# Two attention layers on one core: stacks of 28 rows in four row groups, and scores of one four of heads set beside the transposed scores of the one before

## The reference, cut to what matters

```python
xn = _layernorm(x)
x = x + attention0(xn) + quantized_ffn(xn)      # biases; 128 -> 512 -> 128 with gelu, blocks of 32 rounded to 3 bits
xn = _layernorm(x)
x = x + attention1(xn) + moe(xn)                # 8 experts, 128 -> 512 -> 128, silu(x wg) * (x wu) @ wd, all summed
# attention: sim = q k^T / sqrt(8), causal;  e = exp(sim - max);  out = (e v) / sum(e);  out @ Wo
```

## Time and profile before

| | us |
|---|---|
| runs | 1624.28, 1640.37, 1633.93; median 1633.93 |
| the profiled execution | 1633.84 |
| its span | 1632.1 |
| its mean granted PE clock | 0.914 of 2.4 GHz |
| PE busy | 1501.3 (92%) |
| PEld / DVE / ACT / POOL busy | 840.4 / 1036.6 / 823.3 / 678.2 |

### The profile page before, as it was taken

The page is one execution under the profiler, slowest core; times in us unless marked ns, Lnnn a source line. Parts: engine busy times, 40 slices in busy tenths (PEclk is TensorE's granted clock), DMA queues, the critical chain, the costliest instruction groups (busy, mean ns, idle before and its releaser), DMA issues. The chain is left out here.

```text
span 1632.1 us, 23537 instructions
## 1 busy us (share of the span) xinstructions
PE 1501.3 (92%) x8440; PEld 840.4 (51%) x8440; DVE 1036.6 (64%) x2379; ACT 823.3 (50%) x1220; POOL 678.2 (42%) x791
## 2 busy tenths in 40 slices
PE   2899999999999999369999999999999999999987
PEld 1444444444444443245656656666666566666655
DVE  3545655565655453157876767777777677777743
ACT  2335455555545445135655556555655565555650
POOL 4222324243333223245554455454545554545440
PEclk9559888898979789679999999999999999999997
DMA  3312223232413221231010110111111101111003
GB/s 118 85 35 74 73 82 93 68 98 71 125 56 106 79 64 61 72 92 54 28 52 27 31 47 28 34 48 36 32 53 32 43 28 35 32 37 32 18 14 111
DMA packets 59025, 93.95 MB, mean 58 GB/s; under 512 B 12119, under 2 KB 22876, under 8 KB 56862
## 3 DMA queue, kind: packets, MB, share of 16 engines
q1 hardware_dynamic: 57902, 92.00, 18.9%
q10 hardware_dynamic: 1008, 0.46, 0.1%
HBM read 50.08 MB, written 40.11 MB: 55 GB/s over the span
## 5 line engine op out<-in xcount | busy, mean ns | idle before, releaser
L1133 POOL TENSOR_TENSOR a_h_lo<-a_h,a_h_hi 128x512 fp32r<-128x512 f32 x256 | 329.2, 1286 | 143.6 <-ACT a_h_hi L1180 134.2
L668 DVE TENSOR_REDUCE l_mx<-bank_pair 128x2 f32<-128x1024 f32 (+1 forms) x192 | 200.0, 1044 | 237.7 <-PE bank_pair L886 236.5
L1241 DVE SCALAR_TENSOR_TENSOR a_h<-a_h,bank_pair 128x512 f32<-128x512 f32 x256 | 175.6, 686 | 171.9 <-ACT a_h L1176 169.0
L749 ACT ACTIVATE l_E<-bank_pair 128x1024 f32<-128x1024 f32 (+1 forms) x192 | 169.3, 883 | 179.3 <-PE bank_pair L139 178.8
L192 POOL TENSOR_SCALAR_AFFINE_SELECT l_E<-l_E 128x256 f32<-128x256 f32 (+1 forms) x192 | 95.6, 500 | 382.0 <-ACT l_E L749 382.0
L1187 ACT ACTIVATE a_E<-bank_pair 128x1024 f32<-128x1024 f32 (+1 forms) x192 | 169.8, 884 | 166.5 <-PE bank_pair L139 166.3
L168 DVE CUSTOM_DVE_ANT_0 bank_pair<-bank_pair,mask 128x512 f32<-128x512 f32 (+3 forms) x512 | 238.0, 516 | 7.1 <-PE bank_pair L129 6.9
L1180 ACT ACTIVATE a_h_hi<-a_h 128x512 fp32r<-128x512 f32 x256 | 160.6, 627 | 115.5 <-DVE a_h L1247 115.5
L192 POOL TENSOR_SCALAR_AFFINE_SELECT a_E<-a_E 128x256 f32<-128x256 f32 (+1 forms) x192 | 95.0, 495 | 281.6 <-ACT a_E L1187 281.5
L1247 DVE TENSOR_TENSOR a_h<-a_h,bank 128x512 f32<-128x512 f32 x256 | 176.0, 688 | 27.0 <-DVE a_h L1241 0.5
L1176 ACT ACTIVATE a_h<-bank_pair 128x512 f32<-128x512 f32 x256 | 151.6, 592 | 72.8 <-PE bank_pair L1319 69.2
(11 more groups left out here) (134 smaller groups left out, 2379.1 us busy)
## 6 DMA issues: line engine op xcount, KB each, us to landing
st<-stack_d SPq DMA_DIRECT2D x112, 128.0 KB, 3.1
st<-stack_d SPq DMA_DIRECT2D x224, 64.0 KB, 3.0
stack_d<-l_q_k_hi SPq DMA_DIRECT2D x48, 256.0 KB
stack_d<-l_q_k_lo SPq DMA_DIRECT2D x32, 256.0 KB
o_d<-l_O SPq DMA_DIRECT2D x32, 256.0 KB, 2.0
o_d<-a_O SPq DMA_DIRECT2D x32, 256.0 KB, 2.0
l_st<-stack_d SPq DMA_DIRECT2D x16, 128.0 KB, 3.6
l_st<-stack_d SPq DMA_DIRECT2D x32, 64.0 KB, 3.5
```

The source lines that it names most:

```text
L668: nc.vector.tensor_reduce(out, src, AX.X, ALU.max).then_inc(S_used, 1)
L749: nc.scalar.activation(E[:, pair % SLOTS_E, at_col:at_col + HALVES * w].rearrange("p (r c) -> p r c", r=HALVES), pair_of("T", g, n)[:, :, ...
L1133: nc.gpsimd.tensor_tensor(h_lo[:, q % RH, :], h[:, q % RH, :], h_hi[:, q % RH, :].bitcast(F32), ALU.subtract).then_inc(h_lo_ready, 1)
L1241: nc.vector.scalar_tensor_tensor(hq, hq, 1.0, g_bank[:, :], ALU.add, ALU.mult).then_inc(silu_ready, 1)
```

## The change

A stack half now has 24 rows (three slots, for the products high by high, low by high and high by low; low by low is left out) and the 4 rows of maxima. Two fours share a tile: four g lies at rows 64r + 32(g mod 2). A tile of four stacks is thus two tensors in both layers. A load of a stack is one DMA for each half, two instead of six; the stores of parts are six a batch instead of five. Both kinds of scores are now 24- and 28-row matmuls, and those of four g+1 and four g use different row groups.

In both layers one function sets unit n of S(g+1) and a unit of T(g) alternately. In layer 0 all six T(g) stand in step g, beginning with T(g, 0) at its start, and PV(g) follows the maxima rows of g+1 at its end. The last two units of S have one mask matmul for each half instead of two. The maxima rows are fp32r matmuls against an fp32r identity (8 columns) instead of fp32 transposes (72 columns). The feed-forward of a tile comes four steps later (g-1 instead of g+3), that of a batch's first products one batch later, the weights' quantization and the bias parts two and four steps later; the first queries wait for four small loads of their own (`w0_in`). The other engines' lists follow.

```diff
-SLOTS = 4
+SLOTS = 3
-IMAGE_SLOTS = (((0,), (0, 2)), ((1,), (1,)))
+HALF, GROUP = P // 2, P // 4
+IMAGE_SLOTS = (((0, 2), (0, 1)), ((1,), (2,)))
-STACKS, MOE_STACKS = 4, 3
+STACKS, STACKS_A_BUFFER = 4, 2
...
+def row_of(g, r):
+    return HALF * r + GROUP * (g % STACKS_A_BUFFER)
+def buffer_of(stacks, g):
+    return stacks[g // STACKS_A_BUFFER % len(stacks)]
+def load_stacks(sp, stacks, st_d, g, done):
+    image, st = st_d[g // QUADS_A_BATCH, g % QUADS_A_BATCH], buffer_of(stacks, g)
+    for r in range(HALVES):
+        row = row_of(g, r)
+        sp.dma_start(st[row:row + SLOT_ROWS, :, :, :].bitcast(F32), image[SLOT_ROWS * r:SLOT_ROWS * (r + 1)]).then_inc(done, 16)
```

PE in layer 0:

```diff
-            def S(g, n):
...
-            def T(g, n):
...
+            def scores_and_keys(g, n):
+                more, here = in_range(g + 1), in_range(g)
+                if more:
+                    if n == 0:
+                        pe.wait_ge(stack_in[(g + 1) % STACKS], STACK_LOADS * ((g + 1) // STACKS + 1))
...
+                    begin("S", g + 1, n)
+                if here:
+                    if n == 0:
+                        pe.wait_ge(mrow_in, MAX_LOADS * (g + 1))
+                    begin("T", g, n)
+                    keep_warm(nc, pair_of("T", g, n), identb, mask)
+                t = NT - 1 - n % 2 if n < 4 else 5 - n
+                score_blocks = [(n // 2, t, 0)] if n < 4 else [(j, t, j * N // PLANES) for j in range(PLANES)]
+                key_blocks = UNITS[n % 3]
+                for k in range(2):
+                    for r in range(HALVES):
+                        if more and k < len(score_blocks):
+                            scores(nc, pair_of("S", g + 1, n)[:, r, :], stacks, g + 1, r, score_blocks[k], k == 0, False)
+                    for r in range(HALVES):
+                        if here and k < len(key_blocks):
+                            ins = keys_by_queries(nc, pair_of("T", g, n)[:, r, :], stacks, g, r, n // 3, key_blocks[k])
...
+                if more:
+                    blocks, w = len(score_blocks), P * (t + 1)
+                    for r in range(HALVES):
...
+                        ins = nc.tensor.matmul(diagonal, identb[:, :], part, start=False, stop=True)
+                    ins.then_inc(S_ready, 1)
```

A step of PE in layer 0:

```diff
+                scores_and_keys(g, 0)
                 if u == 0 and ok(b + 1):
                     values(0, b + 1)
...
+                scores_and_keys(g, 1)
                 if u == 1 and ok(y2):
                     turn_input(1, y2)
...
+                scores_and_keys(g, 2)
+                if u == 2 and ok(b + 1):
+                    turn_x(b + 1)
+                scores_and_keys(g, 3)
+                scores_and_keys(g, 4)
+                if q is not None:
+                    turn_tile(q, min(b + 2 if u >= 2 else b + 1, B))
+                scores_and_keys(g, 5)
+                if q is not None:
+                    proj(q)
+                if u == 0 and ok(b):
+                    fc(b, 0)
+                    fc(b, 1)
+                if u == 1 and ok(y2):
+                    queries(1, y2)
                 if u == 2 and ok(a):
                     turn_input(0, a)
...
                 if u == 3 and ok(y1):
                     project_attention(y1)
+                if in_range(g + 1):
+                    maxima_rows(g + 1)
+                if in_range(g):
                     for kb in range(NT):
+                        PV(g, kb)
```

ACT at the end of a step of layer 0:

```diff
+                if in_range(g):
+                    exp(g, 5)
                 if u == 1 and ok(y2):
                     parts(1, y2, 0)
+                if u == 2 and ok(a):
+                    copy_xT(0, a)
                 if in_range(g + 1):
                     copy_mrow(g + 1)
+                if u == 0 and ok(b):
+                    gelus(b, 0)
+                    gelus(b, 1)
```

PE in the second layer:

```diff
+            def scores_and_keys(g, n, m):
+                more, here = n is not None and in_range(g + 1), m is not None and in_range(g)
...
+                if here:
+                    if m == 0:
+                        pe.wait_ge(mrow_in, MAX_LOADS * (g + 1))
+                    if g > 0 or m > 0:
+                        pe.wait_ge(exp_done, UNITS_A_QUAD * g + m)
...
+                for k in range(2):
+                    for r in range(HALVES):
+                        if k < len(score_blocks):
+                            if k == 0 and n > 0:
+                                pe.wait_ge(S_used, SCORES * (g + 1) + 2 * n + r - 1)
+                            ins = scores(nc, S_banks[r], stacks, g + 1, r, score_blocks[k], True, True)
...
+                    for r in range(HALVES):
+                        if k < len(key_blocks):
+                            ins = keys_by_queries(nc, T_banks[:, r, :], stacks, g, r, m // 3, key_blocks[k])
...
+                    c = NC * odd + n
+                    scores_and_keys(g, c if c < UNITS_A_QUAD else None, c - 1 if 0 < c <= UNITS_A_QUAD else None)
```

More of the change, by code:

```diff
@@ L121, in spread, with scores, keys_by_queries @@
     return nc.tensor.matmul(bank[:, :], sel[rows, b % 2, :], rden[rows, :], start=True, stop=True)
[L124 to L141, removed]
+def scores(nc, bank, stacks, g, r, block, first, last):
+    j, t, col = block
+    w, st, rows = P * (t + 1), buffer_of(stacks, g), slice(row_of(g, r), row_of(g, r) + SLOT_ROWS)
+    return nc.tensor.matmul(bank[:, col:col + w], st[rows, j, 0, bass.ts(t, P)], st[rows, j, 1, 0:w], start=first, stop=last)
+def keys_by_queries(nc, bank, stacks, g, r, j, block):
+    kb, col = block
+    w, st, rows = width(kb), buffer_of(stacks, g), slice(row_of(g, r), row_of(g, r) + ROWS)
+    return nc.tensor.matmul(bank[:, col:col + w], st[rows, j, 1, bass.ts(kb, P)], st[rows, j, 0, N - w:N], start=True, stop=True)
 def keep_warm(nc, pair, identb, mask):
@@ L236, in put, with scores_and_keys @@
                 order.append(unit)
-        def scores_of(n):
+        def scores_and_keys(n):
             put(("S", g + 1, n), 0 <= g + 1 < QUADS)
-        def transposed(back, n):
-            put(("T", g - back, n), 0 <= g - back < QUADS)
-        scores_of(0)
-        transposed(1, 3)
+            put(("T", g, n), 0 <= g < QUADS)
+        scores_and_keys(0)
         put(("V", 0, b + 1), u == 0 and 0 <= b + 1 < B)
@@ L248, in units_in_order @@
         put(("Q", 0, b + 2), u == 3 and 0 <= b + 2 < B)
-        scores_of(1)
-        transposed(1, 4)
+        scores_and_keys(1)
         put(("X", 1, b - 2), u == 1 and 0 <= b - 2 < B)
@@ L543, in _ @@
                 if in_range(g):
-                    causal(g, 1)
-                    causal(g, 2)
+                    for n in range(2, UNITS_A_QUAD):
+                        causal(g, n)
                 if u == 0 and ok(y2):
@@ L885, in S @@
                     for r in range(HALVES):
-                        ins = nc.tensor.matmul(pair[:, r, at_col + w - P:at_col + w], identb[:, :], mask[:, N - P:N], start=False, stop=True)
-                ins.then_inc(S_ready, 1)
+                        if here and k < len(key_blocks):
+                            ins = keys_by_queries(nc, pair_of("T", g, n)[:, r, :], stacks, g, r, n // 3, key_blocks[k])
+                            if r == HALVES - 1 and k == len(key_blocks) - 1:
+                                ins.then_inc(T_ready, 1)
@@ L893, in maxima_rows @@
                 for t in range(NT):
-                    ins = nc.tensor.transpose(bank[0:M_COLS, bass.ts(t, P)], nm[:, t, :].bitcast(F32), ident[:, :])
+                    ins = nc.tensor.matmul(bank[0:MAXIMA, bass.ts(t, P)], nm[:, t, :], identr[:, :], start=True, stop=True)
                 ins.then_inc(mT_ready, 1)
-            def T(g, n):
-                if n == 0:
-                    pe.wait_ge(mrow_in, MAX_LOADS * (g + 1))
-                begin("T", g, n)
-                keep_warm(nc, pair_of("T", g, n), identb, mask)
-                keys_by_queries(nc, pair_of("T", g, n), st[g % STACKS], n % 3, n // 3).then_inc(T_ready, 1)
             def PV(g, kb):
@@ L925, in queries @@
             def queries(layer, b):
+                if layer == 0 and b == 0:
+                    pe.wait_ge(w0_in, 16 * FIRST_LOADS)
                 pe.wait_ge(xnT_ready[layer], b + 1)
@@ L934, in values @@
             def values(layer, b):
+                if layer == 0 and b == 0:
+                    pe.wait_ge(w_in, 16 * SMALL_LOADS)
                 begin("V", layer, b)
```

276 lines of the change are left out of this document (102 added, 174 removed).

## The result

The changed kernel takes 1792.41 us (median of four runs, 1777.97 to 1797.67), the kernel before 1633.41 on the same chip: a ratio of 1.096, 95% interval 1.089 to 1.103. The forecast was 1795. The kernel before was profiled at its median.

A forecast was written before the change was run, and what follows sets the result against it. The prediction took TensorE, busy 92% of the span, to bound the kernel before. Its sum: 1633.8 + 216 (layer 0) - 40 (second layer) - 15 (start, seam, end) = 1795 us; range 1655 to 1860, the forecast's own 1740 to 1860.

The forecast's parts named there:

- The loop: Layer 0: each unit goes round keep-warm, streams, mask, VectorE's reduce and release; six units take 15.4 us at full clock.
- The maxima's way: Layer 0, once a step: transpose, copy and two loads before keep-warm, with little work beside them; 4.3 us.
- The size of the two halves: Layer 0's step: 21.2 us at full clock, 25.6 us with the clock mostly at half, against 18.62 before.
- Layer 0's signs: Layer 0: maxima rows 25 to 26 us apart, keep-warm reduce-released in nearly every unit, PE busy about 0.75, clock 5 to 7.
- The clock: Layer 0: runs mostly at half clock, such a unit taking 3.51 us; step 25.6 us, +216 us over 31 steps.
- The rival that relied on the rule: Layer 0: the loop is real but the clock holds; step 21.2 us, whole 1659 us, chance 0.17.
- The second layer: Second layer: both kinds of scores overlap in five of eight slots, VectorE limits the gain; 1.3 us a four, -40 us.
- Start, seam, end: Prologue, passage between the layers and end: earlier first store, one product and four loads fewer; -15 us together.
- The third rival: Layer 0: TensorE stays the bound, its waits filled by later units, and the clock holds; whole 1492 us, chance 0.10.

The follow-up runs named there:

- the swapped pairs: The changed kernel with each unit's transposed scores put ahead of the next four's scores in the order in which bank pairs are handed out; 1684.71 us.
- The clock-only run: The changed kernel with two more keep-warms per unit in the scores' bank pair, the one in the loop kept; 1680.91 us.
- the run with the turn moved: The changed kernel with layer 0 in the old order, and the turn of the second layer's input one unit later; 1575.81 us (0.968).

## Why the prediction was right

The time (1792 against 1795) came out right, and the mechanism is shown: a loop through VectorE's reduce, and a clock that falls in it. That the two numbers lie 3 us apart is in part luck. The profiled execution took 1778, 17 less than the forecast, and there the terms miss by -14 (layer 0), -8 (second layer) and +5.5 us (start and seam). The terms:

- **The loop.** Forecast units at full clock 2.66, 2.40, 2.66, 2.40; measured 2.56, 2.32, 2.66, 2.39 in the step shown. A half-clock unit was forecast at 3.51; the third unit of the steps with u = 1, where keep-warm takes 1.06 us, takes 3.52. The doubled reduce and the swapped pairs show that the reduce is in it. The fifth and sixth unit were forecast at 2.76 and 2.48; they take 3.68 and 4.89, because they are reached at half clock and because the turns, the attention's projection and the last of the feed-forward (438.30 to 441.09) lie behind the last scores, where no wait covers them.
- **The maxima's way.** Forecast 4.3, measured 4.70 and, behind query copies, 5.86.
- **The size of the two halves.** Forecast: 2.6 us a step for the loop at full clock (21.2) and 4.4 for the clock, 7.0 together; measured 6.5 together (25.13 in the profile, 25.6 forecast). The clock-only run puts at most 3.24 on the loop and at least 3.27 on the clock. Since its added bursts take time of their own, the forecast's halves may be nearer than these numbers say; how the missing 0.5 divides is open. One part is seen: the forecast let the clock fall in the third unit, and it does so for u = 1 alone, for u = 0 it is the fourth and for u = 2 and 3 mostly the fifth.
- **Layer 0's signs.** TensorE's busy share is 0.75 as forecast, the clock row 6 and 7. Keep-warm is released by the reduce in 136 of 186 units, fewer than "nearly every" one, and by the maxima's load 16 times in 31 steps: in the step shown the product, 3.98 us long at half clock, covers the load. The maxima rows are 25.13 us apart in the mean and 22 to 27.5 singly.
- **The clock.** The Trainium skill, TensorE: Matmul & The Clock Gate, section Why this matters for your kernels, ties its loss to idle gaps between bursts that are longer than all but one here. The trace decides against it: from the first maxima rows of layer 0 to the last, TensorE has one idle gap of 3.89 us, in the first step, and none beyond 2.51 behind it, and the granted clock is 0.67. It fell in a step whose gaps were 0.41, 1.41 and 1.14 us and, in the run with the turn moved, behind one of 0.82; there it stayed down while TensorE was busy throughout. The rival that relied on the rule (1659) is near what the clock-only run shows (1681), whose clock is 0.96.
- **The second layer.** Forecast -1.3 us a four, -40 us; measured -1.48 and -48.1 from its first maxima rows to the end. An ordinary four fell by 1.18 (26.60 to 25.42, forecast 25.3). The rest of the mean lies in the fours behind an expert's loads: six of these take 27.1 to 32.4 us before and 25.7 to 26.7 after, but 25.6 to 30.6 in the clock-only run, whose second layer has the same code, so part of it is chance. The forecast let VectorE take back 0.5 of the 1.1 us due in the sets; between shared and separate row groups 0.23 of TensorE's 0.68 turn into waiting.
- **Start, seam, end.** -15 forecast: start -14.5 (forecast -10), seam between the layers +5.0 instead of -5 (-3 for one product less, -2 for fewer loads). The loads did save 1.4: from the first of them to the first scores 4.59 us (890.12 to 894.71) instead of 5.97. The -3 did not come: SP's stores of layer 1's parts begin 25.9 us after the last maxima rows of layer 0, where it was 23.0, so the seam begins 2.8 later. The step that failed besides is the count of SP's queue: the fewer loads were counted and the sixth store of parts was not. Six stores take 6.48 us before the store of the denominators' inverses, five took 5.14; the last batch's stores lose as much again. And the first four's scores in the second layer, which wait for VectorE alone, take 1.2 longer.

Timeline of SP at the seam, before:

```profile
660.24 0.65 SPq L400 DMA_DIRECT2D stack_d<-l_q_k_hi  x1
...
665.38 1.19 SPq L439 DMA_DIRECT2D rden_d<-l_rden  x1
```

And after:

```profile
850.36 1.33 SPq L395 DMA_DIRECT2D stack_d<-l_q_k_hi  x2
...
856.84 1.19 SPq L434 DMA_DIRECT2D rden_d<-l_rden  x1
```

The third rival (TensorE stays the bound, 1492) was wrong on this order. On the old one TensorE does stay the bound (busy 516.56 of 549.78 us of layer 0), but the savings it counted come out smaller: 27.6 us in layer 0 (forecast 87) and 35.4 in the rest (forecast 55), by the spans of the two traces.

## What to carry to other kernels

Where an in-order engine waits for two buffers before it issues anything, everything behind both waits joins one loop, and the other engine's time is in the period even if its share of the span is low; follow each buffer round the list in which it is handed out before setting two units side by side. A merge of two streams that saves 0.4 us on the array is worth it only where both buffers have long been free. And count what a wait does to the granted clock: two more bursts of matmuls in the wait, with the loop left whole, were worth 97 us here (1778 to 1681). Moving the burst that stood in the loop into the wait was worth 145 (1778 to 1633), by both ways at once.

## What was not expected

Adding useless matmuls to the busiest engine made the kernel faster: 1778 to 1681 us with the loop kept. Outside the loop it was 1633 to 1620, within the spread of runs. In the run with the turn moved, the clock fell behind a gap of 0.82 us and was at 0.50 from 218 us until the step's end at 233, with TensorE at work throughout. With three bursts ahead of the wait and the turn in its old place the same step fell from 21.4 to 18.1 us, though an idle gap of 1.24 us was left in it. Four streams of 24 and 28 rows in different row groups start at the same instant (890.13 twice) and two of them in the same groups 0.28 us apart. The Trainium skill, TensorE: Matmul & The Clock Gate, section Why this matters for your kernels, says that matmuls of few rows in separate row groups run at once; the trace agrees (a set takes 0.43 us instead of 0.66). Of the 0.68 us that TensorE's work in a four fell by, only 0.45 reached the four's length.
